# Masks moved out of the score matmuls: eight contraction rows for the far mask, masking of the exponentials on POOL and DVE for the near ones

## The chip, the cores and the metric

One core of a Trainium2 chip runs the whole program. The metric is the device time of one execution in microseconds (us). The engines are PE (matmul), ACT (activations), DVE (vector), POOL (GpSimd) and SP, which here only issues DMAs; each runs its own instructions in order, and they meet through semaphores.

## The reference, cut to what matters

For each of B = 4 sequences of S = 1024 tokens with D = 256 features, one pre-norm layer is computed, in float32:

```python
xn = _layernorm(x)                            # (4, 1024, 256)
# attention: 16 query heads, 8 key/value heads of 16 features
mask = causal & (local | lm[:, None, :])      # local: i - j < 128; lm: landmark keys, taken by a
                                              # score of norm and diversity (top 337), dilated by 2
scores = q @ k.T * scale + where(mask, 0, -10000)
s = softmax(scores) @ v @ Wo
# FFN with ternary weights, 256 -> 1024 -> 256
g = silu(gelu(xn @ w1_q.T + b1) @ w2_q.T + b2)
out = x + s * g
```

So a pair (query i, key j) counts when j is not behind i's future and is either at most 127 tokens back or a landmark.

## The kernel before

Scores are held transposed, 128 keys on the partitions and 512 queries on the free axis, so that the exponentials can be multiplied with the values at once. A sequence is done in 48 steps `(c, g, kb)` (`STEPS`): c is one of two query chunks of 512, g one of four groups of four heads, kb a block of 128 keys. Chunk 0 has 4 key blocks per group (steps 0 to 15), chunk 1 has 8 (steps 16 to 47; `C1` is 16). In the last four key blocks of a group a step covers only the queries not ahead of the keys: 512, 384, 256 and 128 columns.

A float32 score is one bf16 matmul: query and key are each split into three bf16 parts, and the six products that matter are stacked along the contraction (`q_stack`, `k_stack`, 96 rows, filled by DMAs on SP's queue, `stack_q`, `stack_k`; three rows more carry the row maximum on a path that this input doesn't take). In step i PE does `scores(i, 0)`, `values(i - 2)`, `scores(i, 1)`, and then side jobs of that step (`jobs_of`): out projections, FFN halves, the projections of the next sequence. `scores(i, u)` writes two heads to PSUM and waits until ACT has read the same half one step earlier. Where a step touches the diagonal, two more matmuls per half add the near masks into PSUM: `mask_ident` (minus 200 on the diagonal) times `near_mask`. Landmarks further back enter as the per-key bias of the exponential, so ACT does two activations where a step has both kinds:

```python
if near > lo:
    last = act.activation(probs[:, i % 3, us, lo:near], sc_ps[:, us, lo:near], ACT.Exp,
                          bias=shift[:, 0:1], scale=HD ** -0.5)
if near < CH:
    last = act.activation(probs[:, i % 3, us, near:CH], sc_ps[:, us, near:CH], ACT.Exp,
                          bias=key_bias[:, kb:kb + 1], scale=HD ** -0.5)
```

Exponentials go to `probs`, three buffers of float32. When a group n ends, DVE copies its result from PSUM (`group_out(n)`, step of the last key block plus 2) once the DMAs `att_group(n - 1)` of the group before have read `att_raw`. SP issues, in this order, in a turn: `spread_rden(0)`, the loads of x, `stack_q(1)`, the output of the turn before, `att_group(0)` to `att_group(3)`, then in chunk 1 `att_group(4)`, `stack_q(0)`, `att_group(5)`, `att_group(6)`, `stack_k`, `att_group(7)`.

A turn handles one sequence and beside it prepares the next: DVE does layer norm (from step `LN_AT`), splits of q and k (chunk 1), token scores, ranks (steps 35 to 42), and PE's `dilate` job at step 44 turns the chosen landmarks into the mask. There is a set-up block, a preparing turn, turn 0, turns 1 and 2 in a loop, and turn 3, which prepares nothing. POOL does the final residual additions (`residual`) and half of the FFN splits, in order of the jobs.

Of the kernel before, what the change touches and what calls it, by code (L numbers as in the profile page):

```python
# [25 lines left out]
def kernel_program(nc, x, Wq, Wk, Wv, Wo, w1, b1, w2, b2, out):  # L26
# [37 lines left out]
    def spans(i):  # L64
        c, _, kb = STEPS[i]
        lo = P * max(0, kb - TC * c)
        return lo, min(CH, max(lo, P * (kb + 2 - TC * c)))

    with ExitStack() as ctx:
# [3 lines left out]
        def sem(name):  # L73
            s = ctx.enter_context(nc.semaphore(name))
            sems.append(s)
            return s

        sems = []
# [8 lines left out]
        NW = 2 * D  # L87
# [10 lines left out]

        xn = sb("xn", [P, T, D])
        xT_hi = sb("xT_hi", [P, KD, S], F32R)  # L100
        xT_lo = sb("xT_lo", [P, KD, S], F32R)
        q_parts = sb("q_parts", [P, QT, 3, S], BF16)
        k_parts = sb("k_parts", [P, 3, S], BF16)
        q_stack = sb("q_stack", [P, H, S], BF16)
        k_stack = sb("k_stack", [P, KVH, S], BF16)
        v_sb = sb("v_sb", [P, T, KVH * VW + 32 - VW])
        probs = sb("probs", [P, 3, NQ, CH])
        near_mask = sb("near_mask", [P, T, P], BF16)
        mask_ident = sb("mask_ident", [P, P], BF16)
# [12 lines left out]
        resid = sb("resid", [P, CH])
# [31 lines left out]

        dve_chain, pool_chain = sem("dve_chain"), sem("pool_chain")
        w1_in, w2_in, wqkv_in, wo_in, b_in, x_in = (sem(n) for n in ("w1_in", "w2_in", "wqkv_in", "wo_in", "b_in", "x_in"))
# [31 lines left out]
        def clear_semaphores():  # L188
            with nc.Block(no_gpsimd_drain=True) as block:  # L189
                @block.sync  # L190
                def _(sp):
# [896 lines left out]
```

## Time and profile before

| | us |
|---|---|
| median of 3 runs | 735.6 (735.58 to 736.71) |
| the profiled execution | 737.96 |
| its span (first to last instruction) | 736.3 |
| busy in the span: PE / ACT / DVE / POOL | 628.7 / 475.7 / 375.4 / 74.7 |
| PE, of it near-mask matmuls (L725) | 105.1 |
| DMA engines' mean busy share by the queue that SP issues to | 33.6% |

The busy time is the sum over an engine's instructions. Matmuls overlap in PE, so the busy time of one kind is more than the time that its removal frees. The busy share alone doesn't say what bounds: that is read stage by stage from the order of the instructions in time.

### The profile page before, as it was taken

To read this page: it belongs to the slowest core of one execution; us is meant where nothing else is said; L and a number is where in the kernel's file an instruction comes from. 1 tells how busy PE (TensorE), PEld (TensorE's weight loads), DVE (VectorE), ACT (ScalarE), POOL (GpSimd) and SP (SyncE) were. 2 spreads that over 40 slices of the span, in tenths; PEclk is the share of its full clock that TensorE was granted. 3 is DMA by queue.
4 is the path that set the end of the run, shared out by engine and by line. 5 is a ranking of instruction groups with operands and counts; after the bars stand their busy time and mean duration, and the time that the engine had idled before them with its cause. 6 is when DMAs were issued, how large, how long until landed. Compare 5 with 4: busy or idle time off the path is not lost. (4 is left out here: it accounts for less than half of the span.)

```text
span 736.3 us, 11753 instructions
## 1 busy us (share of the span) xinstructions
PE 628.7 (85%) x4336; PEld 351.7 (48%) x4336; DVE 375.4 (51%) x1002; ACT 475.7 (65%) x723; POOL 74.7 (10%) x92
## 2 busy tenths in 40 slices
PE   0537809999999989999999679999999899799982
PEld 0524604664455546654554536654554556334532
DVE  7968961665827434767454615648364521410101
ACT  1112417677877766697768556697768666888680
POOL 4000020020010201020100301110100210201001
PEclk9968957999999979999999869999999899899997
DMA  7000699000145659001190756001082691030101
GB/s 214 0 0 1 83 89 153 9 8 20 47 62 77 73 116 144 16 8 31 35 124 21 83 143 102 11 8 58 16 115 37 80 137 42 7 90 8 52 10 49
DMA packets 46833, 43.84 MB, mean 60 GB/s; under 512 B 6065, under 2 KB 41394, under 8 KB 46770
## 3 DMA queue, kind: packets, MB, share of 16 engines
q1 hardware_dynamic: 44642, 41.18, 33.6%
q10 hardware_dynamic: 2128, 1.84, 0.8%
q8 instruction: 38, 0.62, 0.4%
q14 instruction: 25, 0.20, 0.1%
HBM read 11.28 MB, written 4.19 MB: 21 GB/s over the span
## 5 line engine op out<-in xcount | busy, mean ns | idle before, releaser
L812 ACT ACTIVATE probs<-sc_ps,shift 128x512 f32<-128x512 f32 (+1 forms) x288 | 175.8, 617 | 102.0 <-PE sc_ps L725 101.3
L718 PE MATMUL sc_ps<-q_stack,k_stack 99*128 99x512 bf16 (+3 forms) x768 | 198.5, 344 | 33.3 <-PEq L189 14.7
L815 ACT ACTIVATE probs<-sc_ps,key_bias 128x1024 f32<-128x1024 f32 (+3 forms) x256 | 204.9, 818 | 16.5 <-PE sc_ps L718 15.8
L738 PE MATMUL att_ps<-probs,v_sb 128*32 128x512 f32 (+3 forms) x1536 | 167.4, 508 | 0.0
L718 PEld LDWEIGHTS sc_ps<-q_stack,k_stack 99*128 99x128 bf16 x768 | 50.2, 99 | 182.9 <-issue 70.8
L725 PE MATMUL sc_ps<-near_mask,mask_ident 128*128 128x256 bf16 (+1 forms) x576 | 105.1, 266 | 0.0
L850 POOL TENSOR_TENSOR h_lo<-hid,h_hi 128x512 fp32r<-128x512 f32 x32 | 43.2, 1350 | 342.3 <-DVE h_hi L882 342.3
L725 PEld LDWEIGHTS sc_ps<-near_mask,mask_ident 128*128 128x128 bf16 x576 | 56.4, 103 | 37.5 <-issue 7.1
L665 PE MATMUL aux_ps<-w2T,h_hi 128*128 128x256 f32 x256 | 70.1, 307 | 0.0
L665 PE MATMUL aux_ps<-w2T,h_lo 128*128 128x256 f32 x256 | 63.2, 279 | 0.0
L773 ACT ACTIVATE hid<-aux_ps,b_sb 128x512 f32<-128x512 f32 x64 | 42.9, 687 | 22.8 <-PE aux_ps L655 13.8
L655 PE MATMUL aux_ps<-xT_hi,w1T 128*128 128x512 f32 x128 | 53.9, 421 | 4.2 <-ACT hid L773 4.1
L738 PEld LDWEIGHTS att_ps<-probs,v_sb 128*32 128x32 f32 x1536 | 30.5, 109 | 47.6 <-issue 31.7
L996 DVE COPY att_raw<-att_ps 128x512 f32<-128x512 f32 x32 | 22.1, 691 | 60.6 <-PE att_ps L738 40.3
L894 DVE TENSOR_TENSOR gate<-aux_ps,b_bc 128x256 f32<-128x256 f32 x32 | 13.6, 424 | 74.8 <-PE aux_ps L665 53.0
L882 DVE CAST h_hi<-hid 128x512 fp32r<-128x512 f32 x64 | 30.7, 492 | 40.7 <-ACT hid L773 40.5
L655 PE MATMUL aux_ps<-xT_lo,w1T 128*128 128x512 f32 x128 | 50.4, 394 | 0.0
L665 PEld LDWEIGHTS aux_ps<-w2T,h_hi 128*128 128x128 f32 x256 | 48.1, 188 | 1.9
L665 PEld LDWEIGHTS aux_ps<-w2T,h_lo 128*128 128x128 f32 x256 | 48.3, 189 | 0.3
L902 DVE TENSOR_TENSOR gate<-aux_ps,gate 128x256 f32<-128x256 f32 x32 | 13.6, 424 | 61.2 <-PE aux_ps L673 61.2
L673 PE MATMUL aux_ps<-wo_sb,attT 128*128 128x256 f32 x128 | 34.0, 401 | 10.3 <-DVE attT L1008 10.3
L846 POOL TENSOR_TENSOR xn<-xn,gate 128x256 f32<-128x256 f32 x20 | 14.6, 731 | 221.0 <-DVE gate L902 220.8
(152 smaller groups left out, 748.9 us busy)
## 6 DMA issues: line engine op xcount, KB each, us to landing
q_stack<-q_parts SPq DMA_DIRECT2D x96, 128.0 KB, 8.1
k_stack<-k_parts SPq DMA_DIRECT2D x24, 256.0 KB, 8.8
xn<-in_L_attn_hidden_states SPq DMA_DIRECT2D x4, 1024.0 KB, 8.2
attT<-att_raw SPq DMA_DIRECT2D x128, 32.0 KB
rden_bc<-den SPq DMA_DIRECT2D x64, 64.0 KB
probs<-in_L_ffn_w SPq DMA_DIRECT2D x2, 1024.0 KB, 7.8
out_y<-xn SPq DMA_DIRECT2D x4, 512.0 KB, 6.1
xn<-in_L_attn_hidden_states SPq DMA_DIRECT2D x3, 512.0 KB, 4.0
```

The lines of the kernel that those rows point to most:

```text
L655: last = pe.matmul(ps, w1T[:, k, f * P:(f + 1) * P], part[:, k, c * CH:(c + 1) * CH], start=(k == 0 and part is xT_hi), stop=(k == KD - 1 ...
L665: last = pe.matmul(ps[:, 0:D], part[:, f, q * P:(q + 1) * P], w2T[:, f, :], start=(f == 0 and part is h_hi), stop=(f == FT - 1 and part is ...
L673: last = pe.matmul(ps[:, 0:D], attT[:, k, q * P:(q + 1) * P], wo_sb[:, k, :], start=(k == 0), stop=(k == KD - 1))
L718: last = pe.matmul(sc_ps[:, 2 * u + hh, lo:CH], k_stack[0:KROWS + SHIFT_ROWS, h // REP, kb * P:(kb + 1) * P], q_stack[0:KROWS + SHIFT_ROWS ...
L725: last = pe.matmul(sc_ps[:, 2 * u + hh, lo:near], mask_ident[:, :], near_mask[:, first:end:kb + 1, :], start=False, stop=True)
L738: last = pe.matmul(att_ps[32 * q:32 * q + 32, n % 2, lo:CH], v_sb[:, kb, j * VW:j * VW + 32], probs[:, i % 3, q, lo:CH], start=(kb == 0), ...
L773: act.activation(hid[:, u % NHID, :], ps, ACT.Gelu, bias=b1_sb[:, f:f + 1]).then_inc(aux_free[bank], 1)
L812: last = act.activation(probs[:, i % 3, us, lo:near], sc_ps[:, us, lo:near], ACT.Exp, bias=shift[:, 0:1], scale=HD ** -0.5)
L815: last = act.activation(probs[:, i % 3, us, near:CH], sc_ps[:, us, near:CH], ACT.Exp, bias=key_bias[:, kb:kb + 1], scale=HD ** -0.5)
L850: pool.tensor_tensor(h_lo[:, f, :], hid[:, u % NHID, :], h_hi[:, f, :].bitcast(F32), ALU.subtract).then_inc(hid_split_pool, 1)
L882: ins = dve.tensor_copy(h_hi[:, f, :], whole)
L996: dve.tensor_copy(att_raw[:, :], att_ps[:, n % 2, :]).then_inc(att_out, 1)
```

## The change

The 576 near-mask matmuls go. The stacks get eight rows more (104 instead of 99 take part): on the query side row r holds 32768 in the query tiles that lie two or more behind tile r, on the key side row r holds, for the keys of tile r, landmark minus 1. One contraction thus adds minus 32768 to scores with keys in far tiles that are no landmarks. The diagonal block is zeroed after the exponential by POOL (`causal`), and the block next to it is multiplied by `near` (1 where the key is in the window or a landmark) by DVE in chunk 0 and by POOL in chunk 1 (`local`). `values(i)` stays two steps behind and now waits for these as well. ACT does one activation per half. The rows for the key side are made from the landmarks by a new job (`far_rows`) and a DMA (`fill_far`). The key stack is filled group by group (`fill_k`), and each stacking DMA is cut: 24 of 64 KB for a query chunk instead of 12 of 128 KB, 24 of 64 KB for the keys instead of 6 of 256 KB. Layer norm, the inverse root and the token scores are spread over the steps differently. The whole kernel exists twice now, once for inputs that need exact row maxima and once (`fast_path`) for the others; one branch behind set-up chooses. `fast_path` begins with a block of its own that fills pads and the query side's eight rows.

The core of the diff, its indentation cut (the new lines are those of `fast_path`):

```diff
+LN_AT, ROOT_AT, NORMAL_AT = 3, 7, 10
-LN_AT = 5
-jobs += [(s1 + 28, "dilate")]
+jobs += [(s1 + 28, "dilate"), (s1 + 29, "far_rows")]
 def stack_q(c):
     cs = slice(c * CH, (c + 1) * CH)
     for i in range(NPART):
-        for m in range(QT):
-            sp.dma_start(q_stack[i * HD:(i + 1) * HD, m * HT:(m + 1) * HT, cs],
-                         q_parts[:, m, QPART[i], cs]).then_inc(stack_in[c], 16)
+        for g in range(H // NQ):
+            sp.dma_start(q_stack[i * HD:(i + 1) * HD, g * NQ:(g + 1) * NQ, cs],
+                         q_parts[half_rows(g), g // QT, QPART[i], cs]).then_inc(stack_in[c], 16)
+def fill_k(g):
+    sp.wait_ge(k_split, NC)
+    if main:
+        sp.wait_ge(sc_done, 2 * (GROUP_END[GROUPS + g] + 1))
+    for i in range(NPART):
+        sp.dma_start(k_stack[i * HD:(i + 1) * HD, 2 * g:2 * g + 2, :],
+                     k_parts[g * 2 * HD:(g + 1) * 2 * HD, KPART[i], :]).then_inc(kstack_in, 16)
 att_group(4)
 if prep:
+    fill_k(0)
     sp.wait_ge(q_split, 2)
     stack_q(0)
 att_group(5)
+if prep:
+    fill_k(1)
 # scores(i, u)
-last = pe.matmul(sc_ps[:, 2 * u + hh, lo:CH], k_stack[0:KROWS + SHIFT_ROWS, ...
+last = pe.matmul(sc_ps[:, 2 * u + hh, lo:CH], k_stack[0:KROWS + T, ...
-if near > lo:
-    first = 0 if has_tri(i) else kb + 1
-    end = kb + 2 if has_local(i) else 1
-    for hh in range(2):
-        last = pe.matmul(sc_ps[:, 2 * u + hh, lo:near], mask_ident[:, :], near_mask[:, first:end:kb + 1, :],
-                         start=False, stop=True)
 # values(i)
 pe.wait_ge(exp_done, 2 * (i + 1))
+if has_tri(i):
+    pe.wait_ge(tri_done, TRIS[i])
+if has_local(i):
+    pe.wait_ge(local_done, LOCALS[i])
 # exps(i)
+act.activation(probs[:, i % 3, us, lo:CH], sc_ps[:, us, lo:CH], ACT.Exp,
+               bias=shift[:, 0:1], scale=HD ** -0.5).then_inc(exp_done, 1)
 # POOL
+def causal(i):
+    pool.wait_ge(exp_done, 2 * (i + 1))
+    pool.affine_select(out=block_probs, in_=block_probs, compare_op=ALU.is_ge, fill=0.0, base=0,
+                       pattern=[[0, NQ], [1, P]], channel_multiplier=-1).then_inc(tri_done, 1)
+def local(i):
+    pool.wait_ge(exp_done, 2 * (i + 1))
+    pool.tensor_tensor(block_probs, block_probs, near[:, kb, :].unsqueeze(1).to_broadcast([P, NQ, P]),
+                       ALU.mult).then_inc(local_done, 1)
+for i in range(NSTEP + LAG):
+    for _, kind, *a in jobs_at(i - 0.5, i + 0.5):
+        job(kind, *a)
+    if i < NSTEP and has_tri(i):
+        causal(i)
+    if C1 <= i < NSTEP and has_local(i):
+        local(i)
 # DVE, step i
+if main and 1 <= i <= C1 and has_local(i - 1):
+    local(i - 1)
-if prep and LN_AT <= i < LN_AT + T // 2 + 1:
+if prep and LN_AT <= i < LN_AT + T // 2:
     if i == LN_AT:
         dve.wait_ge(x_in, 16)
+# the pads of fast_path
+lk(pool.memset(later_tile, FAR_UNIT))
+lk(pool.affine_select(out=later_tile, in_=later_tile, compare_op=ALU.is_ge, fill=0.0, base=-2,
+                      pattern=[[1, T], [0, P]], channel_multiplier=-1))
+sp.dma_start(q_stack[KROWS:KROWS + T, :, :], later_tile.unsqueeze(1).to_broadcast([T, H, S])).then_inc(stack_in[0], 16)
```

On SP's queue, in the looped turn (1 and 2), from its start. Before:

```order
L586 DMA rden_bc<-den 128x1x128 [waits rden_done]
L586 DMA rden_bc<-den 128x1x128 x7
L597 DMA hid<-in_L_attn_hidden_states 128x4x256
L599 DMA xn<-in_L_attn_hidden_states 128x8x256
L561 DMA q_stack<-q_parts 16x8x512 x12
L603 DMA out_y<-hid 128x4x256 [waits y_done]
L578 DMA attT<-att_raw 16x512 [waits aux_done,att_out]
L578 DMA attT<-att_raw 16x512 x3
L579 DMA den<-att_raw 16x1x128
```

The same place in the changed kernel:

```order
L1264 DMA f_q_stack<-f_q_parts 16x4x512 x24
L1317 DMA out_y<-f_hid 128x4x256 [waits f_y_done]
L1292 DMA f_attT<-f_att_raw 16x512 [waits f_aux_done,f_att_out]
L1292 DMA f_attT<-f_att_raw 16x512 x3
L1293 DMA f_den<-f_att_raw 16x1x128
```

The order is the same, but 24 issues instead of 12 stand ahead of the DMAs of `att_group(0)`.

On DVE, in a turn that prepares, steps 9 to 11 (L1748 is `group_out(1)`, L1612 `local`, L1634 an FFN job's addition); the changed kernel:

```order
L1612 TENSOR_TENSOR f_probs<-f_probs,f_near 128x4x128 [waits f_exp_done,f_dve_chain]
L1634 TENSOR_TENSOR f_gate<-aux_ps,b_bc 128x256 [waits f_aux_done]
L1748 COPY f_att_raw<-att_ps 128x512 [waits f_z_done,f_att_in,f_pv_done]
L151 COPY rstd<-root 128x8
L1612 TENSOR_TENSOR f_probs<-f_probs,f_near 128x4x128 [waits f_exp_done,f_dve_chain]
L1694 TENSOR_SCALAR xn<-xn,mv,rstd 128x256 x2
```

Before, DVE had no `local`; now the masking of step 9 (the second L1612) stands behind `group_out(1)` and its wait for `att_in`.

On POOL, in chunk 1 of such a turn, before:

```order
L850 TENSOR_TENSOR h_lo<-hid,h_hi 128x512 x4
L846 TENSOR_TENSOR xn<-xn,gate 128x256 x4
L850 TENSOR_TENSOR h_lo<-hid,h_hi 128x512 x4
```

The changed kernel, from step 23 (the last key block of group 0 of the chunk) to step 29; L1572 is `causal`, L1579 `local`, L1561 `residual`:

```order
L1572 AFFINE_SELECT f_probs<-f_probs 128x4x128 [waits f_exp_done]
L1561 TENSOR_TENSOR xn<-xn,f_gate 128x256 [waits f_prod_done,f_xres_in]
L1579 TENSOR_TENSOR f_probs<-f_probs,f_near 128x4x128 [waits f_exp_done]
L1572 AFFINE_SELECT f_probs<-f_probs 128x4x128 [waits f_exp_done]
L1579 TENSOR_TENSOR f_probs<-f_probs,f_near 128x4x128 [waits f_exp_done]
L1561 TENSOR_TENSOR xn<-xn,f_gate 128x256 [waits f_prod_done]
L1572 AFFINE_SELECT f_probs<-f_probs 128x4x128 [waits f_exp_done]
L1579 TENSOR_TENSOR f_probs<-f_probs,f_near 128x4x128 [waits f_exp_done]
```

So in steps 27 and 29 the masks that `values` waits for stand behind a residual addition, which waits for DVE's product and, the first time, for the load of x.

## Rows read from the trace of the kernel before

**Rows 1.** Windows: us, busy PE, PEld, DVE, ACT, POOL; granted clock, DMA share, GB/s.

```profile
261.07:264.20 3.13, 0.04 (x1) 0.00 (x0) 0.21 (x1) 1.07 (x5) 0.00 (x0) 0.73 0.03 4
264.20:272.40 8.20, 8.05 (x29) 2.66 (x30) 1.25 (x2) 6.21 (x10) 0.00 (x0) 0.50 0.25 73
264.20:427.10 162.90, 151.39 (x1071) 84.30 (x1071) 88.07 (x244) 117.13 (x177) 16.76 (x16) 0.95 0.38 63
```

**Rows 2.** Chain that ended last, turn 3: start, us, what.

```profile
685.65 0.22 PE sc_ps L725 x2
```

**Rows 3.** Timeline of ACT and PE, end of group 3 in turn 1, chunk 1: start, us.

```profile
397.52 0.68 ACT L815 ACTIVATE probs<-sc_ps,key_bias 128x512 f32<-128x512 f32 x1
399.79 0.47 ACT L815 ACTIVATE probs<-sc_ps,key_bias 128x256 f32<-128x256 f32 x1
...
399.74 1.07 PE L738 MATMUL att_ps<-probs,v_sb 128*32 128x512 f32 x8
401.50 0.85 PE L738 MATMUL att_ps<-probs,v_sb 128*32 128x384 f32 x8
```

**Rows 4.** POOL's groups by form: busy us, mean ns, idle ahead.

```profile
L850 POOL TENSOR_TENSOR h_lo<-hid,h_hi 128x512 fp32r<-128x512 f32 x32 | 43.2, 1350 | 342.3 <-DVE h_hi L882 342.3
L269 POOL MEMSET v_sb<- 128x1208 f32 x1 | 1.1, 1113 | 0.0
L273 POOL TENSOR_SCALAR_AFFINE_SELECT ident<-ident 128x128 f32<-128x128 f32 x1 | 0.3, 295 | 0.5 <-POOL den L269 0.5
```

**Rows 5.** Timeline, DVE and POOL in the FFN stretch of turn 1.

```profile
312.06 0.69 DVE L887 TENSOR_TENSOR h_lo<-hid,h_hi 128x512 fp32r<-128x512 f32 x1
313.46 1.67 DVE L887 TENSOR_TENSOR h_lo<-hid,h_hi 128x512 fp32r<-128x512 f32 x1
...
313.17 1.41 POOL L850 TENSOR_TENSOR h_lo<-hid,h_hi 128x512 fp32r<-128x512 f32 x1 [1.43 <-DVE h_hi L882]
```

**Rows 6.** Timeline of SP's queue, turn 1, chunk 0: start, us of issuing, issues.

```profile
271.45 0.37 SPq L599 DMA_DIRECT2D xn<-in_L_attn_hidden_states  x1
271.87 8.07 SPq L561 DMA_DIRECT2D q_stack<-q_parts  x12
...
283.27 2.56 SPq L578 DMA_DIRECT2D attT<-att_raw  x4
```

**Rows 7.** DMA issues, 264 to 300 us: KB each, median us from issue to landing.

```profile
xn<-in_L_attn_hidden_states SPq DMA_DIRECT2D x1, 1024.0 KB, 7.9
```

**Rows 8.** Timeline of DVE and PE, turn 1, chunk 0.

```profile
277.32 0.42 DVE L902 TENSOR_TENSOR gate<-aux_ps,gate 128x256 f32<-128x256 f32 x1 [4.00 <-PE aux_ps L673]
293.53 0.69 DVE L996 COPY att_raw<-att_ps 128x512 f32<-128x512 f32 x1 [0.84 <-DMA den<-att_raw]
...
295.27 0.85 PE L738 MATMUL att_ps<-probs,v_sb 128*32 128x384 f32 x8
```

**Rows 9.** Timeline of POOL, PE, SP and DVE, turn 1, chunk 1.

```profile
355.72 0.74 POOL L846 TENSOR_TENSOR xn<-xn,gate 128x256 f32<-128x256 f32 x1 [36.54 <-DVE gate L902]
...
355.54 1.06 PE L738 MATMUL att_ps<-probs,v_sb 128*32 128x512 f32 x8
...
368.02 8.27 SPq L561 DMA_DIRECT2D q_stack<-q_parts  x12
...
390.70 0.69 DVE L996 COPY att_raw<-att_ps 128x512 f32<-128x512 f32 x1 [0.21 <-DVE gate L894]
395.37 0.18 DVE L990 TENSOR_SCALAR lm_pad<-score_t 128x8 bf16<-128x8 f32 x1
...
396.73 0.22 PE L706 MATMUL aux_ps<-lm_pad,band 128*128 128x8 bf16 x3
```

**Rows 10.** Timeline of DVE in the set-up block.

```profile
11.12 6.88 DVE L299 MEMSET k_stack<- 32x8192 bf16 x1 [1.66 <-issue]
18.04 2.29 DVE L304 TENSOR_REDUCE wsum<-probs 128x8 f32<-128x2048 f32 x1
25.28 0.15 DVE L319 TENSOR_SCALAR thr<-aux_ps 128x2 f32<-128x2 f32 x1
```

More of the change, by code:

```diff
@@ L67, in spans @@
         return lo, min(CH, max(lo, P * (kb + 2 - TC * c)))
+    FAR_UNIT = 32768.0
+    NW = 2 * D
     with ExitStack() as ctx:
@@ L71, in sb, with named @@
             return ctx.enter_context(nc.sbuf_tensor(name, shape, dt))
[L73 to L78, printed above, removed]
+        def named(names, group):
+            for n in names.split():
+                group.append(ctx.enter_context(nc.semaphore(n)))
+            return group[-len(names.split()):]
         ident = sb("ident", [P, P])
@@ L186, in link @@
             return f
[L188 to L191, printed above, removed]
-                    lo = min(s.num for s in sems)
-                    assert [s.num for s in sems] == list(range(lo, lo + len(sems)))
-                    sp.sem_clear(range(lo, lo + len(sems)))
         def rsqrt(dve, lk, m):
@@ L435, in _ @@
                     @block.tensor
                     def _(pe):
-                        for h in range(H):
-                            if h >= 2:
-                                pe.wait_ge(masked_done, h - 1)
-                            for half in range(NC):
-                                last = pe.matmul(sc_ps[:, 2 * (h % 2) + half, :], q_stack[:, h, bass.ds(t * P, P)],
-                                                 k_stack[:, h // REP, half * CH:(half + 1) * CH], start=True, stop=True)
-                            last.then_inc(sc_done, 1)
@@ L444, in _ @@
-                        pe.wait_ge(max_done, 1)
-                        pe.transpose(aux_ps[0:H, 0, 0:P], row_max, ident[:, :]).then_inc(max_row_done, 1)
+                        pe.wait_ge(consts_done, 1)
+                        pe.wait_ge(wabs_done, 2)
+                        pe.matmul(aux_ps[:, 0, 0:2], ones[:, :], wsum[:, :, T], start=True, stop=True).then_inc(wtotal_done, 1)
+                        pe.wait_ge(wnat_split, 1)
+                        for n, w in enumerate((w_nat, wk_rep)):
+                            for m in range(QT):
+                                for k in range(KD):
+                                    last = pe.matmul(aux_ps[:, 1, (QT * n + m) * P:(QT * n + m + 1) * P], w[:, k, m * P:(m + 1) * P],
+                                                     w[:, k, m * P:(m + 1) * P], start=(k == 0), stop=(k == KD - 1))
@@ L455, in _ @@
-                        for h in range(H):
-                            dve.wait_ge(sc_done, h + 1)
-                            ps = sc_ps[:, 2 * (h % 2):2 * (h % 2) + 2, :].rearrange("p a n -> p (a n)")
-                            dve.tensor_tensor(masked, ps, mask, ALU.add).then_inc(masked_done, 1)
-                            dve.wait_ge(masked_done, h + 1)
-                            lk(dve.tensor_reduce(row_max[:, h:h + 1], masked, AX_X, ALU.max))
-                        dve.tensor_scalar(row_max, row_max, -1.0, None, ALU.mult).then_inc(max_done, 1)
@@ L462, in _ @@
[L462 to L466 removed]
+                        dve.wait_ge(pads_done, 1)
+                    @block.tensor
@@ L1067 @@
+        set_up()
+        exact = nc.values_load(exact_flag[0:1, 0:1], min_val=0, max_val=1)
+        with nc.If(exact != 0):
+            general_path()
+        with nc.Else():
+            fast_path()
 _INS = ["L0_attn_hidden_states", "L0_attn_Wq", "L0_attn_Wk", "L0_attn_Wv", "L0_attn_Wo",
```

2199 lines of the change are left out of this document (1432 added, 767 removed).

## The prediction, made before the run

> **What bounds the kernel now.** I read the windows of the stages first: in turn 1 PE is busy for 151.39 of 162.90 us, ACT for 117.13, DVE for 88.07 and POOL for 16.76 [rows 1]. So PE sets the pace where it has work, and what the change takes from PE is worth its full length there, as long as nothing that PE waits for comes later. I then went through the order in time for the places where PE waits or nearly waits. There are four kinds, and the forecast hangs on them. First, `values(i)` against the exponentials: at the end of a group of chunk 1 the last activation of step 44 ends at 397.52 + 0.68 = 398.20 and `values(44)` starts at 399.74, so 1.54 us lie between; for step 45 it is 401.50 - 400.26 = 1.24 us [rows 3]. Second, SP issues a DMA each 0.64 to 0.67 us whatever its size: 12 of 128 KB in 8.07 us, 4 of 32 KB in 2.56 [rows 6]. Third, DVE's `group_out(1)` already waits 0.84 us for the DMAs of `att_group(0)` [rows 8]. Fourth, PE's `dilate` at 396.73 needs `lm_pad`, which DVE starts at 395.37: 1.2 us of room after its 0.18 [rows 9].
>
> **What the change removes.** In the chain that ended last, a half's pair of near-mask matmuls (256 columns each) costs 0.22 us [rows 2]; I take 0.11 for 128 columns, by width. A group of chunk 0 has three steps with two wide pairs and one step with narrow ones: 3 x 0.44 + 0.22 = 1.54 us. A group of chunk 1 has one narrow step more: 1.76. Four groups each give 6.2 + 7.0 = 13.2 us a turn, 53 us in four turns, if PE could use all of it. ACT does one activation less in each masked half (such a second one took 0.68 and 0.47 us [rows 3]); ACT is off the path, so I add nothing for it, and allow up to 0.3 us a group in the range.
>
> In set-up, the second of DVE's two memsets of pads ends at 18.00 and the reduction of the weights starts at 18.04; the threshold follows at 25.28 [rows 10]. Without them the reduction waits for the weights' load alone. I take 9.8 for it, near the end of the first memset (11.12 - 1.66 = 9.46, where the gap that no other engine ends begins). That is -8.2 us for the threshold, and between 0 and -15 at most.
>
> **What it adds on POOL.** `local` on 128x512 float32 is the nearest to POOL's L850 of the same shape: 1.35 us [rows 4]. `causal` selects in 128x512: the 128x128 selection takes 0.295 us. With a fixed part of about 0.1 this gives 0.1 + 4 x 0.195 = 0.88. Lower bound by the slope of a memset (1208 columns in 1.113 us): 0.1 + 512 x 0.84 ns = 0.53; upper bound, that of the two-input operation: 1.35. I take 0.88, since the same operation is the nearer row. So steps with both kinds (kb 4 to 6 of chunk 1) occupy POOL for 2.23 us, bounds 1.9 and 2.7, and a group of chunk 1 for 3 x 2.23 + 1.35 + 0.88 = 8.9 us. Against room of 1.24 to 1.54 at the end of a group without side jobs [rows 3], two such steps cost PE about 0.7 and 1.0 us, and the third, shorter one 1.2, for POOL is behind by then: 2.9 us. The gain there is 1.76, so the last group of chunk 1 becomes 1.1 us slower. In steps with an FFN job between (room about 2.5 by the same reading, since PE's step is longer by the job) POOL keeps up and the gain of 1.5 to 1.76 stands.
>
> **What it adds on DVE.** `local` of chunk 0 is 12 operations a turn. Alone, L887, a two-input operation of this shape, takes 0.69 us; beside POOL's L850 it took 1.67 and ended at 315.13, after POOL's end at 314.58 [rows 5]. So a two-input operation of DVE may wait for a running operation of POOL: with 12 to 16 causal operations about, 0.7 to 1.7 each. The Trainium skill ("SBUF — State Buffer", section "Who interferes with whom") says that a DVE instruction with two inputs in SBUF and a GpSimd one that reads SBUF exclude each other for a whole instruction; this trace agrees (0.69 against 1.67 us).
>
> **The queue of SP.** `stack_q` becomes 24 issues, 24 x 0.65 = 15.6 us, 7.5 more [rows 6]. In turns 1 to 3 `att_group(0)` is thus issued from about 288.5 instead of 283.27 [rows 6], ending at about 291.7, and its data land no sooner than the 293.5 at which `group_out(1)` starts now [rows 8]. PE gets there earlier than now, but gains nothing: `local(9)` stands behind `group_out(1)` on DVE, so `values(9)` starts at 293.5 + 0.69 + 0.7 plus hand-over, about 295.3, against 295.27 now. All of the gain of the nine steps ahead, 3.6 us, is lost there. From there DVE has to fit locals, layer norm's products and the gates of `ffn_down` before `ffn_up`: 0.7 us more in each of six steps, +4.2. And layer norm now starts at step 3 instead of 5, with a wait for x ahead of the gates of `out_proj`: the load is issued at 271.45 and needs 7.9 us to land, 279.4 [rows 6, 7]; two pieces of layer norm later the gates that DVE did at 277.32 [rows 8] come at about 281. That wait lies within the first steps, whose gain is lost already. For turns 1 and 2 chunk 0 comes to -6.2 + 3.6 + 4.2 = +1.6, say +1.5 (bounds -6.2, if none of it holds, and +3, if the ports double). Turn 0 has no `out_proj` of a turn before ahead of it, and I leave it half of its gain, -3; turn 3 prepares nothing and keeps what the queue doesn't take, -2.6 and some port time, -2.
>
> **Chunk 1.** In turns that prepare, the first three groups gain 3 x 1.76 = 5.3. Three things go against it. `residual` stands ahead of `local(27)` on POOL; it now starts at 355.72, in the same stretch as `values(27)` at 355.54 [rows 9], so that DVE's product, POOL's 0.74 and a local of 1.35 come in sequence, 1.5 us later than PE wants them; DVE's operations beside POOL's cost about as much again: +3.0 (bounds 0 and 5). Before `att_group(5)` SP issues 6 for `fill_k(0)` and 24 for `stack_q(0)`, 30 x 0.65 = 19.5 us, where 8.27 did [rows 9]: 368.0 + 19.5 + 5 x 0.65 = 390.7, landing about 393. `group_out(6)`, now at 390.70, waits for that on DVE, with the last ranks behind it: `lm_pad` moves from 395.37 to about 398.5. PE would reach `dilate` at 396.7 - 5.3 + 3.0 = 394.4 and stands until 398.7: +4.3 (bounds 0 and 6). The last group costs 2.9 - 1.76 = +1.1, as above. Sum: -5.3 + 3.0 + 4.3 + 1.1 = +3.1. Turn 3 has no ranks, but two groups without FFN jobs (2 x 1.1) and two in which a little is left over: +2.
>
> **Set-up and preparing.** The new block runs alone: POOL's memset of 1208 columns is 1.11 us [rows 4], one of 1024 about 0.95, a selection of 1024 columns 0.1 + 8 x 0.195 = 1.7, the small ones 0.6: 4.4. Then 256 KB go by DMA to eight partitions with everything waiting: 1024 KB land in 7.9 us [rows 7], so 256 KB on few partitions take 3 to 7; I take 6.5. Block end, clearing of semaphores and the branch: about 4 (bounds 1.7 and 6; turn changes cost 3.13 us of an idle PE [rows 1], with more in them). That is 15 against the -8.2: +6.8. `fill_far` at the end of the preparing turn adds an issue and a landing to the keys' path: 0 to 2, say +1.
>
> **The sum** against the profiled 737.96: +6.8 +1.0, turn 0 -3 + 3.1 = +0.1, turns 1 and 2 each 1.5 + 3.1 = +4.6, together +9.2, turn 3 -2 + 2 = 0. This gives 755.1; the profiled execution is 2.4 above the median of 735.6, so **753**.
>
> **Rivals.** *Same gain, no new waits.* If `causal` takes under 0.6 us, or the exponentials come early enough since ACT has less to do, `values` never waits, and if DMAs of 64 KB land sooner than those of 128 KB, `group_out` isn't late either. Then 53 us are had against 7.8 of set-up: 738 - 53 + 8 - 2 = 691; with half of the gain eaten, 718; a range of 691 to 730, and it ends on the other side of no change. For it speaks that PE is the bound by 151 of 163 us [rows 1]; against it, the room of 1.24 to 1.54 us [rows 3]. It decides where POOL's two operations and hand-overs stay under about 1.5 us at the end of a group. The Trainium skill ("GPSIMD Engine Reference", section "4.1 Engine selection") advises against two-input elementwise work on GpSimd, as about 2 times slower than VectorE; the rows agree (1.35 against 0.69 us), and it speaks for waits.
>
> *Stalls bring the clock down.* After PE had been idle for 3.13 us its clock was granted at 0.50, which is 1.2 of 2.4 GHz, for the next 8.20 us [rows 1]. If stalls of 2 to 4 us in the middle of a turn (at `group_out(1)`, at `dilate`) do the same, each costs up to half of 8.2, 4.1 us; two in three turns and some after: +9 to +20, so 762 to 775.
>
> *Near no change.* Set-up's cost is half as large, and gains and waits balance: 731 to 741.
>
> **How the numbers follow.** The forecast, waits that give the gain back plus a set-up that grows: 0.50, 742 to 764. The gain holds: 0.27. The clock: 0.13. Near balance: 0.10, of which 0.04 within 0.2% (1.5 us, about what a measurement tells here from no change), 0.03 on each side. Faster 0.30, same 0.04, slower 0.66. The range leaves out the lower half of the second case (0.14) and the end of the third (0.04): 718 to 772.
>
> **What would show it.** Right: the first instruction of the preparing turn starts at about 52 instead of 44.9; PE idle before `values` with POOL as releaser at kb 4 to 6 of the last groups, 0.7 to 1.2 us each; SP's 24 issues take over 15 us; `group_out(1)` waits for the DMA; turns about 0, 5, 5 and 0 us longer than now (162.9 was turn 1 [rows 1]). Wrong: turns of 145 to 150 us with no such waits, a `causal` far from 0.88 us, or a new block that costs 5 us.

## The result

The changed kernel takes 767.9 us (median of 4 runs, 760.2 to 771.5) against 735.6 before: ratio 1.042, 95% interval 1.034 to 1.050. It is slower. The forecast was 753, range 718 to 772: the sign was right, the size was 17 us of 32. The main case of the forecast had 742 to 764; the measured time lies outside it and inside the 762 to 775 of its rival on the clock.

The windows of the profile after, a stage each (set-up and preparing turn, turns 0 to 3): busy PE, PEld, DVE, ACT, POOL, then granted clock, DMA share, GB/s.

```profile
0.00:119.18 119.18, 51.55 (x212) 41.66 (x213) 74.96 (x231) 24.59 (x50) 14.52 (x32) 0.74 0.24 64
119.18:279.64 160.46, 143.31 (x912) 72.14 (x913) 97.36 (x247) 109.62 (x137) 54.26 (x60) 0.90 0.24 55
279.64:449.02 169.38, 146.36 (x929) 75.33 (x929) 102.71 (x253) 110.92 (x137) 57.79 (x64) 0.90 0.28 61
449.02:617.68 168.66, 147.88 (x929) 76.05 (x929) 101.03 (x253) 109.04 (x136) 57.97 (x64) 0.90 0.27 61
617.68:769.70 152.02, 120.51 (x784) 54.00 (x784) 38.87 (x60) 96.12 (x111) 57.26 (x64) 0.89 0.19 50
```

Before, the same five took 110.0, 154.2, 162.9 [rows 1], 156.9 and 152.3 us, with 0.92 to 0.97 of the clock in the turns. PE's busy time fell by 19 us only, from 628.7 to 609.6. In the four turns it was busy for 558.1 us at 0.89 to 0.90 of its clock, where experiment 4 below, with the same matmuls and no masking, has 535.1 at 0.92 to 0.96; between its matmuls it stood idle for 92.5 us, 43.8 before. The profile by waits (engine, tile, line, what it waited for: us in total, times, the longest) names waits that have to do with the change; 7.6 of the 20.0 us lie in the preparing turn, where the kernel before has them too:

```profile
DVE f_att_raw L1748 <- DMA f_den<-f_att_raw: 31.9, 9, 4.5
PE att_ps L1458 <- POOL f_probs L1579: 25.1, 19, 4.2
PE aux_ps L1426 <- DVE f_lm_pad L1742: 20.0, 4, 7.6
PE att_ps L1458 <- DVE f_probs L1612: 10.1, 8, 2.2
```

POOL's groups (busy us, mean ns, idle ahead of them) show that its operations were cheaper than I took them to be, 1165 ns for `local` and 746 for `causal`:

```profile
L1572 POOL TENSOR_SCALAR_AFFINE_SELECT f_probs<-f_probs 128x512 f32<-128x512 f32 x128 | 95.4, 746 | 164.6 <-ACT f_probs L1531 164.6
L1579 POOL TENSOR_TENSOR f_probs<-f_probs,f_near 128x512 f32<-128x512 f32 x64 | 74.6, 1165 | 107.2 <-ACT f_probs L1531 107.2
```

The longest wait of `values` for a mask, 4.20 us, stands at the same place in turns 0, 1 and 2: at `values(29)`, in the second group of chunk 1. Timelines of ACT, POOL and PE there in turn 1:

```profile
373.60 0.90 ACT L1531 ACTIVATE f_probs<-sc_ps,shift 128x768 f32<-128x768 f32 x1 [1.01 <-PE sc_ps L1441]
...
370.77 1.15 POOL L1579 TENSOR_TENSOR f_probs<-f_probs,f_near 128x512 f32<-128x512 f32 x1
371.87 0.63 POOL L1572 TENSOR_SCALAR_AFFINE_SELECT f_probs<-f_probs 128x512 f32<-128x512 f32 x1
372.48 1.15 POOL L1579 TENSOR_TENSOR f_probs<-f_probs,f_near 128x512 f32<-128x512 f32 x1
377.70 0.72 POOL L1561 TENSOR_TENSOR xn<-xn,f_gate 128x256 f32<-128x256 f32 x1 [4.07 <-DVE f_gate L1642]
378.38 0.63 POOL L1572 TENSOR_SCALAR_AFFINE_SELECT f_probs<-f_probs 128x512 f32<-128x512 f32 x1
378.98 1.15 POOL L1579 TENSOR_TENSOR f_probs<-f_probs,f_near 128x512 f32<-128x512 f32 x1
...
380.28 1.51 PE L1458 MATMUL att_ps<-f_probs,f_v_sb 128*32 128x384 f32 x8 [4.20 <-POOL f_probs L1579]
```

The exponentials of step 29 are complete at 374.50. POOL is idle for 4.07 us, to 377.70, all the same: a `residual` (L1561) stands first and waits for DVE's product. The masks follow only at 378.38, and PE, idle since 376.08 (380.28 - 4.20), starts `values(29)` at 380.28. What held DVE up is on its own timeline:

```profile
370.03 0.17 DVE L129 TENSOR_TENSOR root_t<-root_in,root 128x9 f32<-128x9 f32 x1
370.24 0.59 DVE L130 TENSOR_TENSOR root_t<-root_t,root 128x9 f32<-128x9 f32 x1
370.86 1.08 DVE L131 SCALAR_TENSOR_TENSOR root<-root_t,root 128x9 f32<-128x9 f32 x1
371.98 0.55 DVE L129 TENSOR_TENSOR root_t<-root_in,root 128x9 f32<-128x9 f32 x1
372.56 1.10 DVE L130 TENSOR_TENSOR root_t<-root_t,root 128x9 f32<-128x9 f32 x1
373.69 0.17 DVE L131 SCALAR_TENSOR_TENSOR root<-root_t,root 128x9 f32<-128x9 f32 x1
```

Operations on 9 columns, 0.17 us each, take 0.55 to 1.10 beside POOL, which masks from 370.77 to 373.63. The first long one ends at 370.83, behind the first residual (370.80), and the other three at 371.94, 372.53 and 373.66, each 0.02 or 0.03 us behind the end of a mask (371.92, 372.50, 373.63). The four take 3.32 us instead of 0.68, and the product that `residual` waits for is behind them, at 377.21, although its matmuls had ended at 374.43. So of the 4.20 us up to 2.6 are this stretching (an estimate). The ring closes: POOL's masks slow DVE, DVE's product comes late, and POOL's next masks stand behind it.

### The profile page after: what moved, and what is told of

Read it like the earlier page. It is cut to its first block and busy times, and to the rows that moved or that the text cites. A ratio compares the mean times of both kernels' runs of the same rounds, so it can differ in the third digit from the quotient of the medians.

```text
span 769.7 us, 11049 instructions
## 1 busy us (share of the span) xinstructions
PE 609.6 (79%) x3764; PEld 319.2 (41%) x3764; DVE 414.9 (54%) x1041; ACT 450.3 (58%) x568; POOL 241.8 (31%) x284
## 5 line engine op out<-in xcount | busy, mean ns | idle before, releaser
L1531 ACT ACTIVATE f_probs<-sc_ps,shift 128x1024 f32<-128x1024 f32 (+3 forms) x384 | 332.6, 902 | 162.0 <-PE sc_ps L1441 160.0
L1441 PE MATMUL sc_ps<-f_q_stack,f_k_stack 104*128 104x512 bf16 (+3 forms) x768 | 200.1, 355 | 28.5 <-ACT f_probs L1531 12.1
L1458 PE MATMUL att_ps<-f_probs,f_v_sb 128*32 128x512 f32 (+3 forms) x1536 | 178.8, 539 | 35.9 <-POOL f_probs L1579 25.1
L1572 POOL TENSOR_SCALAR_AFFINE_SELECT f_probs<-f_probs 128x512 f32<-128x512 f32 x128 | 95.4, 746 | 164.6 <-ACT f_probs L1531 164.6
L1441 PEld LDWEIGHTS sc_ps<-f_q_stack,f_k_stack 104*128 104x128 bf16 x768 | 51.7, 101 | 199.5 <-ACT f_probs L1531 120.6
L1579 POOL TENSOR_TENSOR f_probs<-f_probs,f_near 128x512 f32<-128x512 f32 x64 | 74.6, 1165 | 107.2 <-ACT f_probs L1531 107.2
L1385 PE MATMUL aux_ps<-w2T,f_h_hi 128*128 128x256 f32 x256 | 72.6, 317 | 0.0
L1385 PE MATMUL aux_ps<-w2T,f_h_lo 128*128 128x256 f32 x256 | 63.4, 281 | 0.0
L1493 ACT ACTIVATE f_hid<-aux_ps,b_sb 128x512 f32<-128x512 f32 x64 | 43.8, 690 | 30.0 <-PE aux_ps L1375 24.2
L1375 PE MATMUL aux_ps<-f_xT_hi,w1T 128*128 128x512 f32 x128 | 59.3, 463 | 0.7 <-ACT f_hid L1493 0.7
L1622 DVE CAST f_h_hi<-f_hid 128x512 fp32r<-128x512 f32 x64 | 33.2, 532 | 44.3 <-ACT f_hid L1493 44.1
L1375 PE MATMUL aux_ps<-f_xT_lo,w1T 128*128 128x512 f32 x128 | 55.5, 433 | 0.0
L1612 DVE TENSOR_TENSOR f_probs<-f_probs,f_near 128x512 f32<-128x512 f32 x48 | 35.1, 738 | 36.8 <-ACT f_probs L1531 35.9
L1748 DVE COPY f_att_raw<-att_ps 128x512 f32<-128x512 f32 x32 | 22.1, 691 | 56.4 <-DMA f_den<-f_att_raw 31.9
L1561 POOL TENSOR_TENSOR xn<-xn,f_gate 128x256 f32<-128x256 f32 x20 | 14.6, 732 | 88.2 <-DVE f_gate L1642 75.9
```

Source lines behind the costliest of these rows:

```text
L1375: last = pe.matmul(ps, w1T[:, k, f * P:(f + 1) * P], part[:, k, c * CH:(c + 1) * CH], start=(k == 0 and part is xT_hi), stop=(k == KD - 1 ...
L1385: last = pe.matmul(ps[:, 0:D], part[:, f, q * P:(q + 1) * P], w2T[:, f, :], start=(f == 0 and part is h_hi), stop=(f == FT - 1 and part is ...
L1441: last = pe.matmul(sc_ps[:, 2 * u + hh, lo:CH], k_stack[0:KROWS + T, h // REP, kb * P:(kb + 1) * P], q_stack[0:KROWS + T, h, c * CH + lo:( ...
L1458: last = pe.matmul(att_ps[32 * q:32 * q + 32, n % 2, lo:CH], v_sb[:, kb, j * VW:j * VW + 32], probs[:, i % 3, q, lo:CH], start=(kb == 0), ...
L1493: act.activation(hid[:, u % NHID, :], ps, ACT.Gelu, bias=b1_sb[:, f:f + 1]).then_inc(aux_free[bank], 1)
L1531: act.activation(probs[:, i % 3, us, lo:CH], sc_ps[:, us, lo:CH], ACT.Exp, bias=shift[:, 0:1], scale=HD ** -0.5).then_inc(exp_done, 1)
```

## The experiments

All times are medians, each beside runs of the kernel before on the same chip (medians of 736 to 738 us there), and each ratio is to those, with its 95% interval. "The changed kernel" is 767.9 us, with 760.2 to 771.5 from run to run.

**1. POOL's masks ahead of its jobs**

```diff
 for i in range(NSTEP + LAG):
+    if i < NSTEP and has_tri(i):
+        causal(i)
+    if C1 <= i < NSTEP and has_local(i):
+        local(i)
     for _, kind, *a in jobs_at(i - 0.5, i + 0.5):
         job(kind, *a)
-    if i < NSTEP and has_tri(i):
-        causal(i)
-    if C1 <= i < NSTEP and has_local(i):
-        local(i)
```

> The changed kernel, with one order turned round: on POOL the masks of a step stand ahead of the jobs of that step (residual additions, FFN splits) instead of behind them. Theory (POOL's order): in the trace of the changed kernel a residual that waits for DVE's product stands ahead of the masks of steps 27, 29, 31, and PE then waits 4.2 us for values in the second group of chunk 1; without it 4 to 5 us are had in each of four turns, 748 to 756 us. Rival (the lower granted clock of PE, 0.876 against 0.935, costs the time and the stalls only add a little): under 5 us are had, 763 us or more.

758.9 us (755.2 to 761.1), ratio 1.029 (1.024 to 1.034). 9 us are had (3 to 17 by the two intervals), less than 12 to 20 and more than 5, so neither expectation holds in full. The longest wait of PE for POOL falls from 4.2 to 3.0 us, but the sum of them only from 25.1 to 19.1:

```profile
PE att_ps L1458 <- POOL f_probs L1579: 19.1, 19, 3.0
PE att_ps L1458 <- DVE f_probs L1612: 14.0, 11, 3.9
```

The wait has moved by a step. `values(29)` waits 0.40 us now, but the residual of step 29 stands ahead of the masks of step 30 and still waits for DVE, and `values(30)` waits 2.95 or 2.96 us for them in turns 0, 1 and 2. Turn 1, POOL and PE:

```profile
372.07 0.73 POOL L1561 TENSOR_TENSOR xn<-xn,f_gate 128x256 f32<-128x256 f32 x1 [2.94 <-DVE f_gate L1642]
372.75 0.64 POOL L1572 TENSOR_SCALAR_AFFINE_SELECT f_probs<-f_probs 128x512 f32<-128x512 f32 x1
...
374.66 0.85 PE L1458 MATMUL att_ps<-f_probs,f_v_sb 128*32 128x256 f32 x8 [2.96 <-POOL f_probs L1579]
```

**2. Twelve DMAs of 128 KB for a query chunk again**

```diff
-for g in range(H // NQ):
-    sp.dma_start(q_stack[i * HD:(i + 1) * HD, g * NQ:(g + 1) * NQ, cs],
-                 q_parts[half_rows(g), g // QT, QPART[i], cs]).then_inc(stack_in[c], 16)
+for m in range(QT):
+    sp.dma_start(q_stack[i * HD:(i + 1) * HD, m * HT:(m + 1) * HT, cs],
+                 q_parts[:, m, QPART[i], cs]).then_inc(stack_in[c], 16)
```

The heads of a tile land in another order than the weights' columns have here, so the numbers computed differ; the work is the same. (The waits that count these DMAs follow.)

> The changed kernel with the query stack filled by 12 DMAs of 128 KB a chunk again, instead of 24 of 64 KB. Theory (SP's issues): group_out waits 31.9 us in all for the DMAs of att_group in the changed kernel, most of it behind 15 to 17 us of issuing; with half the issues 2 to 4 us are had in each of five places, so 753 to 762 us. Rival (the bytes set the landing, not the issues): within 3 us of the changed kernel.

753.7 us (752.1 to 756.4), ratio 1.023 (1.019 to 1.028): 14 us (7 to 21 by the intervals), the size that the theory gave, but not where it gave it. From the turn's first scores to the first `ffn_up` after chunk 0 turns 1 and 2 take 45.3 and 44.3 us, against 44.3 and 44.3 in the changed kernel: nothing is had there. `group_out(1)` of these turns did not wait for DMAs in the changed kernel either (experiment 5 shows why). The profiled executions differ by 5.8 us up to turn 0, 6.7 in turn 0, 0.0 in turn 1, 2.0 in turn 2 and 2.4 in turn 3; of the 6.7, 3.9 are PE's busy time, at 0.93 of its clock instead of 0.90. The preparing turn's part is PE's clock, not the DMAs (below).

**3. The kernel before without its near-mask matmuls**

```diff
-if near > lo:
-    first = 0 if has_tri(i) else kb + 1
-    end = kb + 2 if has_local(i) else 1
-    for hh in range(2):
-        last = pe.matmul(sc_ps[:, 2 * u + hh, lo:near], mask_ident[:, :], near_mask[:, first:end:kb + 1, :],
-                         start=False, stop=True)
```

> The kernel before without the 576 near-mask matmuls; nothing replaces them, so the causal and local masks are missing from the scores. The rest, two activations per masked half too, is as before. It prices the gain that the change goes for. By the sum of the forecast it is 53 us: 683 us. Rival (other engines or their order take over early, ranks on DVE above all): 700 to 725 us.

697.0 us (695.0 to 698.2), ratio 0.946 (0.942 to 0.949): the matmuls are worth 39 us, where the sum said 53, and the measurement lies just below the rival's range. The turns become 10.9, 9.6, 11.0 and 9.7 us shorter, not 13.2. PE's busy time in them fell by 51.2 us, but it stands idle for 10.0 more (53.8 against 43.8). Over the whole execution its weight loads wait more for ACT: 88.4 us behind L808, the second activation, against 64.7 before.

**4. The changed kernel without any masking of the exponentials**

```diff
-    if i < NSTEP and has_tri(i):
-        causal(i)
-    if C1 <= i < NSTEP and has_local(i):
-        local(i)
...
-if has_tri(i):
-    pe.wait_ge(tri_done, TRIS[i])
-if has_local(i):
-    pe.wait_ge(local_done, LOCALS[i])
...
-if main and 1 <= i <= C1 and has_local(i - 1):
-    local(i - 1)
```

> The changed kernel without the masking on POOL and DVE and without values' wait for it; the diagonal and local masks are left out of the result, the far mask stays. It prices all that the masking costs, waits and ports. If waits for the masks take the gain (the forecast): 700 to 715 us, that is 50 to 65 less than the changed kernel. If the queue of SP, the serial block and the clock take it: 735 us or more.

708.8 us (706.5 to 712.2), ratio 0.964 (0.960 to 0.968): the masking costs 59 us, in the range expected if waits for masks take the gain. In the profiled executions the four turns are 60.4 us shorter than in the changed kernel: 37.4 of them are time in which PE stood idle, and 23.0 are PE's busy time, the same matmuls at a higher clock (busy time times clock is 501 us there and 503 here, an estimate from the windows). Everything else in the change (queue, serial block, larger program, one activation less) costs 709 - 697 = 12 us beside experiment 3. So the removed matmuls give 39 us, the masking on POOL and DVE takes 59, and the rest 12.

**5. Layer norm from step 5 again** (`LN_AT, ROOT_AT, NORMAL_AT = 5, 9, 12` for `3, 7, 10`)

> The changed kernel with layer norm on DVE from step 5 again (inverse root from 9, normalising from 12) instead of 3, 7 and 10. Theory: in turns 1 and 2 the first group_out is 3 us later than before (20.8 against 17.8 us after the turn's first scores), since DVE waits for the load of x at step 3 ahead of the gates of out_proj, and halving SP's issues did not change that; the wait is had back: 2 to 3 us in each of turns 1 and 2, 762 to 764 us. Rival (DVE's later steps bind, and the shift crowds normalising into steps 12 to 15): no gain, 766 us or more.

768.7 us (764.7 to 775.0), ratio 1.045 (1.039 to 1.052): no gain, the number of the rival. The wait is had back, `group_out(0)` of turns 1 and 2 comes 15.6 us after the first scores instead of 20.8 and 21.0, and is gone again at `ffn_up`: 46.2 and 46.7 us instead of 44.3. Most of it is lost in one place, before the later steps that the rival named: `group_out(1)`, early now, waits for the DMAs of `att_group(0)`, `local(9)` stands behind it, and PE waits for that (turn 1; 3.70 us for the DMA in turn 2):

```profile
303.55 0.69 DVE L1748 COPY f_att_raw<-att_ps 128x512 f32<-128x512 f32 x1 [4.33 <-DMA f_den<-f_att_raw]
...
306.21 1.51 PE L1458 MATMUL att_ps<-f_probs,f_v_sb 128*32 128x384 f32 x8 [4.82 <-DVE f_probs L1612]
```

In the changed kernel `group_out(1)` of these turns has no such wait (0.21 us, on DVE itself). So the wait for x and the wait for 24 issues hide each other: experiments 2 and 5 each remove one of them and gain nothing there.

**6. Values three steps behind, ahead of the scores of their step**

```diff
+LAGF = 3      # for LAG in the path that runs; ffn_up's tail jobs stay where they were
 for i in range(NSTEP + LAGF):
+    if i >= LAGF:
+        values(i - LAGF)
     if i < NSTEP:
         scores(i, 0)
-    if i >= LAG:
-        values(i - LAG)
     if i < NSTEP:
         scores(i, 1)
```

The loops of POOL and DVE and the step of `group_out` follow LAGF. Nothing else is edited, and the exponentials keep their three buffers.

> The changed kernel with values three steps behind instead of two, ahead of the scores of its step, on the same three buffers of exponentials. It gives POOL about half a step and the side jobs more. Theory (latency of POOL's masks at the end of groups, 25 us of PE waiting for local and more in the shorter waits): 750 to 757 us. Rival (order on POOL and DVE, where a mask stands behind a residual that waits, is longer than half a step, and the exponentials now start later in each step): 764 us or more.

731.4 us (728.7 to 732.3), ratio 0.991 (0.988 to 0.994). One edit takes 36.5 us off and makes the change a gain of 0.9%; I had expected 11 to 18. The edit moves `values` in two ways, a step further behind and ahead of the scores of its step; which of the two gives how much was not separated. Its rows of waits:

```profile
PE aux_ps L1427 <- DVE f_lm_pad L1743: 12.8, 4, 7.6
PE att_ps L1459 <- POOL f_probs L1580: 10.8, 8, 3.0
```

And its windows of turns 0 to 3, columns as above:

```profile
113.63:264.92 151.29, 137.98 (x912) 69.95 (x913) 96.80 (x247) 107.28 (x137) 54.59 (x60) 0.95 0.26 58
264.92:428.23 163.31, 143.06 (x929) 74.61 (x929) 101.08 (x253) 108.59 (x137) 57.50 (x64) 0.93 0.28 63
428.23:585.86 157.63, 142.74 (x929) 74.23 (x929) 99.71 (x252) 106.32 (x136) 57.95 (x64) 0.94 0.30 65
585.86:730.40 144.54, 119.70 (x784) 53.05 (x784) 40.17 (x60) 94.30 (x111) 56.35 (x64) 0.90 0.19 52
```

PE's waits for masks fall from 25.1 + 10.1 to 10.8 us (waits for DVE's `local` are no longer among the 60 largest), and its clock in turns 0 to 2 is 0.93 to 0.95 instead of 0.90. The four turns are 33.7 us shorter: PE is idle for 19.2 us less and busy for 14.6 less, so a part of the gain is the clock. Of the 10.8 us, 9.1 are one wait of 3.0 at `values(29)` in each of turns 0 to 2, behind the residual.

**7. No branch and no second program**

```diff
-with nc.If(exact != 0):
-    general_path()
-with nc.Else():
-    fast_path()
+fast_path()
```

> The changed kernel without the branch and without the program for inputs that need exact row maxima (this input doesn't take it); all that runs is the same. Theory of the forecast: the branch is 1 to 3 us of the 13 between set-up's end and the preparing turn: 765 to 767 us. Rival (the twice as long program costs more, by loading instructions at each change of block): 760 us or less.

759.6 us (757.5 to 763.0), ratio 1.032 (1.029 to 1.036). By the median the rival (8 us, 1 to 14 by the intervals), but the traces don't bear it out as far: from the end of set-up DVE's idle time ahead of its first operation is 12.95 instead of 14.51 us, so the branch is 1.6 us. In the profiled executions 6.5 of 14 us lie before turn 0, most of it PE's clock, and 8.7 in turn 2, where DVE had x 10.4 us after the first scores (15.5 in turn 2 of the changed kernel). What the longer program costs in the turns stays open.

**8. The four edits of 1, 2, 5 and 6 together** (with the query weights' columns arranged for the 12 DMAs, in the path that this input takes)

> The changed kernel with four edits together: POOL's masks ahead of its jobs, 12 DMAs of 128 KB for a query chunk (with the query weights' columns in the order that they need, for the path that this input takes), layer norm from step 5, values three steps behind. If the edits add up (9 and 14 us measured, 4 and 14 expected): 728 to 738 us. If they remove the same waits: 745 us or more.

723.6 us (720.3 to 729.6), ratio 0.985 (0.980 to 0.989). Below the range expected: the third step gives more than I had put in.

**9. Three steps in the kernel before** (the same two edits as in 6)

> The kernel before with values three steps behind, ahead of the scores of its step. A control for e6: if three steps gave the changed kernel 36 us because its values waited for masks on POOL and DVE, the kernel before, whose values waits for ACT alone, gets nothing: 733 to 745 us. Rival (the old order between scores halves was simply worse, also without masks): 715 to 728 us.

746.6 us (745.5 to 747.8), ratio 1.012 (1.010 to 1.014). That is 1.6 us above the range of the control and far from the rival: without masks behind the exponentials the same edit costs 9 us. So the 36 us of experiment 6 come from the room that it gives to the masks, with what the clock gives back for it.

**10. Three steps and 12 DMAs**

> The changed kernel with values three steps behind and the query stack filled by 12 DMAs of 128 KB a chunk (query columns arranged for it on the path that this input takes). Lag alone gave 731.4 us and 12 DMAs alone took 14 off. If SP's queue is a cost of its own: 720 to 726 us. Rival (12 DMAs alone gained mostly by the higher granted clock in the preparing turn, 6 us, and by what lag removes too): 728 us or more.

731.7 us (726.8 to 733.4), ratio 0.990 (0.986 to 0.994), as experiment 6. The profiled execution has its turns 0 to 2 each 1 to 2 us shorter and the preparing turn 5.7 us longer. The 12 DMAs have no gain that the medians show.

**11. Three steps, 12 DMAs, POOL's masks first**

> As e10, with POOL's masks ahead of its jobs too: the combination e8 without the later layer norm. If the residual ahead of a mask still costs with three steps: 715 to 722 us, and below e8's 723.6 if layer norm at 5 cost there; if three steps hide it: as e10, within 3 us.

721.0 us (717.0 to 725.5), ratio 0.977 (0.972 to 0.983). POOL's order is worth 10.6 us also with three steps (4 to 14 by the intervals). Against experiment 8 the earlier layer norm makes no difference that can be told in the medians. In the traces experiment 8 reaches `ffn_up` 37.0 us after the first scores in turns 1 and 2, this one after 42.9 and 39.9: with 12 DMAs and the later layer norm neither of the two waits is left. It loses 2.5 to 4.0 us again between there and the second `ffn_up`, and why stays open.

**12. Three steps and POOL's masks first, 24 DMAs as in the change**

> The changed kernel with values three steps behind and POOL's masks ahead of its jobs, the stack with 24 DMAs as in the change. If the number of DMAs is worth nothing once values has its room (e10 against e6): 718 to 725 us, as e11. If 12 DMAs are still worth some: 727 us or more.

717.8 us (713.9 to 719.4, 6 runs), ratio 0.973 (0.971 to 0.976): the lowest median of all, not told apart from experiment 11, so the 12 DMAs are worth nothing that shows, as expected for that case. It is 50 us below the changed kernel by two edits of order, and 19 below the kernel before. Beside experiment 6, the same but for POOL's order, it gains 13.6 us. PE's waits for POOL:

```profile
PE att_ps L1459 <- POOL f_probs L1580: 6.9, 9, 1.4
```

Its windows of turns 0 and 1:

```profile
113.54:260.44 146.90, 136.18 (x912) 69.46 (x913) 98.49 (x247) 107.27 (x137) 54.65 (x60) 0.96 0.27 60
260.44:417.61 157.17, 141.18 (x928) 73.65 (x929) 103.83 (x253) 108.62 (x137) 57.45 (x64) 0.95 0.30 66
```

## Why the forecast had the sign and half of the size

**The gain.** 53 us were put in for the matmuls' columns; experiment 3 measured 39. The price was right: PE's busy time in the turns fell by 51.2 us. The condition was not, "if PE could use all of it": 10 us came back as idle time of PE. That ACT is what it waits for then is suggested by the rows of waits and not shown.

**The room of values.** The step was right, that two operations of POOL don't fit in 1.24 to 1.54 us [rows 3]; experiments 4, 6 and 9 show it together (59 us of masking, 36 of them given back by a third step, which costs the kernel before 9). I had costed it only in the groups without side jobs, 1.1 us net each. The last group of turn 3, which has no ranks either, went from 13.11 to 13.95 us from one `group_out` to the next, +0.8, with 0.73, 0.21 and 1.30 us of PE's waits for POOL in it: the size was right where it was put. In turn 1 the last group went from 16.0 to 18.5 us, but there the stall at `dilate` lies in it too.

**The clock.** The step that failed: the sum had no term for PE's clock, which stood only among the rivals, with a chance of 0.13. Windows of turn 1 around the wait at `values(29)`, columns as above:

```profile
372.00:376.08 4.08, 4.01 (x28) 1.69 (x28) 3.84 (x8) 2.25 (x4) 1.63 (x2) 1.00 0.00 0
376.08:380.28 4.20, 0.00 (x1) 0.03 (x2) 1.38 (x7) 0.98 (x2) 2.58 (x4) 0.72 0.01 2
380.28:384.00 3.72, 3.72 (x15) 1.81 (x16) 0.04 (x1) 0.48 (x1) 1.56 (x2) 0.50 0.00 0
384.00:388.00 4.00, 4.00 (x29) 1.72 (x28) 0.81 (x2) 2.88 (x3) 2.01 (x3) 0.90 0.00 0
```

PE was busy at 1.00, stood for 4.20 us, and was then granted 0.50 (1.2 of 2.4 GHz) for 3.72 us and 0.90 for the next 4.00. At the full clock the same work would have taken 2.3 us less (an estimate: 3.72 x 0.50 + 4.00 x 0.10). The same follows the waits of 4.20 us in turns 0 and 2 and the stalls of 4.11 or 4.12 us at `dilate` in turns 0 to 2: 0.50 for 3.0 to 4.1 us, then 0.69 to 0.82. By the same estimate the six come to 2.3 to 2.9 us each, 15.7 together. In the kernel before the granted clock is 1.00 in all of turn 1 from 276 to 416 us. The forecast of 753 is 15 us short. The rival had named stalls of 2 to 4 us, at `dilate` and `group_out(1)`, and a price of +9 to +20: right at `dilate`, and the other stall was `values(29)`. That the range held is owed to this rival, since the main case ended at 764.

**The residual ahead of a mask.** The second term that was too small: "in sequence, 1.5 us later than PE wants them", and +3.0 with the ports. `values(27)`, where I had put it, waited 0.56 to 0.58 us; `values(29)` waited 4.20. Together they are 4.8 us, and the second group of chunk 1 grew from 22 to 27 us in each of turns 0 to 2, the clock's part in it. What ended the long wait was the product behind DVE's small operations, four of which took 3 to 6 times their length beside POOL. The load of x has a part in turn 1 only: the first residual waited for it to 370.04, with DVE's product done at 369.88. I had put as much again for DVE's operations beside POOL's as for the order, with the large two-input ones of chunk 0 in mind [rows 5] and not the serial chains of chunk 1. The order alone is 9 us (experiment 1), 10.6 and 13.6 with a third step (11 against 10, 12 against 6).

**Chunk 0.** Up to `ffn_up` it changed by -2.9, +2.4, +2.1 and -0.2 us in turns 0 to 3; the forecast had -3, +1.5, +1.5, -2. For turns 1 and 2 the number is near by luck. 24 issues took 15.32 us in turn 1, as worked out, but `group_out(1)` did not wait for the DMAs there, only in turn 3 (2.91 us), and it is turn 3 that gained 3.1 us with 12 DMAs (experiment 2). What binds in turns 1 and 2 is the wait for x, which I had put at nothing: DVE idles 4.74 and 5.44 us for it, and `group_out(0)` comes 20.8 and 21.0 us after the first scores instead of 17.8 and 18.2. The path that I had worked out lies right behind it and shows when it is gone (experiment 5). In turn 3 it shows too: `values(9)` waits 2.19 us behind that `group_out(1)`. Besides, in turns 0 to 2 `values` waits 2.2 us for DVE's `local` right ahead of `ffn_up`.

**Chunk 1.** Forecast +3.1 in each of three turns; measured +9.2, +4.0 and +9.7, of which 9.8, 8.8 and 10.0 lie between the starts of the two `ffn_up` stretches (before, turn 1 took 24.0 us from the second one to its end, turns 0 and 2 17.5; after, 19.2). That is 6 to 7 us above the forecast; by the sizes above some 5 us a turn are the clock and 1.8 the residual. The stall at `dilate` was sized rightly: (20.0 - 7.6) / 3 = 4.1 us a turn, against 4.3. Turn 3 came out at 0.0 instead of +2.

**Set-up.** The threshold comes at 16.82 instead of 25.28 [rows 10], -8.5 (forecast -8.2). From set-up's end to the first operation of the preparing turn it is 14.5 us instead of 1.65, +12.9 (forecast 15). With 0.3 in the rest of set-up that is +4.7 against +6.8.

**The preparing turn** grew by 4.5, not 1. That is the clock again, at a place that I didn't name. Windows of the changed kernel and of experiment 6, which runs the same instructions there:

```profile
80.00:84.00 4.00, 2.49 (x16) 1.68 (x14) 3.76 (x7) 1.20 (x2) 0.00 (x0) 1.00 0.42 101
84.00:98.00 14.00, 14.00 (x60) 13.03 (x59) 9.22 (x33) 4.80 (x12) 0.00 (x0) 0.51 0.38 99
```

```profile
80.00:84.00 4.00, 2.49 (x22) 2.20 (x21) 3.51 (x7) 1.79 (x3) 0.00 (x0) 1.00 0.41 98
84.00:98.00 14.00, 12.58 (x70) 9.42 (x69) 13.55 (x50) 6.97 (x16) 2.58 (x2) 1.00 0.38 103
```

For 14 us PE is granted 0.51 in the one and 1.00 in the other, and turn 0 starts at 119.18 and at 113.63. Of the profiled executions of this path experiments 1 and 10 fell on the long side too (119.0 and 119.3), the others at 112.7 to 114.6, so this is 5 to 6 us of luck in any single run. The changed kernel's runs lie 11 us apart, and their mean clocks go with their times (0.902 at 760.2 us, 0.876 at 771.5).

Of the other rivals, *near no change* did not come, nor did *same gain, no new waits*, but its deciding point was right: with the room of a third step much of the gain is had.

## What to carry to other kernels

When work moves from an engine's own instructions to another engine behind it, the consumer's distance has to grow with it: price the change with the distance that it needs, not with the one that is there. On an engine that takes on latency-bound work, put that work ahead of jobs that wait for something else in the same step. Price what DVE and POOL cost each other on the small serial chains too, not only on the large operations: here they were stretched most, and POOL waited for their end. And price a stall of PE with the clock behind it: a wait of 4.2 us cost 2 to 3 us more.

## What was not expected of the hardware

Operations on 128x9 elements took 0.55 to 1.10 us instead of 0.17 while POOL ran 1.15 and 0.63 us operations on 128x512, and ended 0.02 or 0.03 us behind POOL's operations. This agrees with the Trainium skill ("SBUF — State Buffer", section "Who interferes with whom"), by which a two-input DVE instruction waits for a whole GpSimd instruction that reads SBUF.

PE's clock fell to 0.51 for 14 us in which PE was busy throughout, after 4 us at 1.00 with 2.49 us busy; in another execution of the same instructions it stayed at 1.00. What decided between them no run here shows. Nor does one show it for stalls: after the same 2.95 or 2.96 us of idle PE in experiment 1 the next 3.4 us were granted 1.00 in turn 0 and 0.54 in turn 1.

POOL's selection of 128x512 took 0.636 us in the median and 0.746 in the mean; all that took more than 0.65 ran beside an operation of DVE. Its product of the same shape took 1.165 us, below the 1.35 of L850 [rows 4].
